# Last pair of attention heads run batch by batch, with separate homes for the second head's K and Q and the first head's output weight

## What is computed

```python
x = x + attn(_layernorm(x), ...)            # 32 heads of 128, K and Q normed over all heads
x = x + xattn(_layernorm(x), ctx_4096, ...) # fake-quantised product with the context
x = x + ffn(_layernorm(x), ...)             # base product + routed low-rank experts

# attn
q = rms_norm(h @ Wq + bq, gq); k = rms_norm(h @ Wk + bk, gk); v = h @ Wv + bv
attn = softmax(einsum('bhqd,bhkd->bhqk', q, k) * scale)
out  = einsum('bhqk,bhkd->bhqd', attn, v)   # 2 batches, 32 heads
return out @ Wo + bo

# xattn, one product per batch
q1 = clip(round(x1 / s1 + z1), 0, 255); q2 = clip(round(x2 / s2 + z2), 0, 255)
return matmul((q1 - z1) * s1, (q2 - z2) * s2)
```

## Time and profile before

| | us |
|---|---|
| median of 3 runs | 537.58 |
| lowest, highest | 535.88, 537.90 |
| the profiled execution | 537.49 |
| its span, first to last instruction | 535.6 |
| mean granted TensorE clock, share of full | 0.996 |

### The profile page before, as it was taken

How to read it: one execution, slowest core, us unless ns; L and a number is a source line. 1 busy time by engine, 2 the same in 40 slices (tenths; PEclk the granted TensorE clock), 3 DMA queues, 4 the chain that set the end, 5 groups by cost and what they waited for, 6 DMA issues and landing times.

```text
span 535.6 us, 9738 instructions
## 1 busy us (share of the span) xinstructions
PE 521.4 (97%) x3213; PEld 462.6 (86%) x3213; DVE 331.6 (62%) x696; ACT 354.8 (66%) x741; POOL 271.0 (51%) x228
## 2 busy tenths in 40 slices
PE   6999999999999999999999999999999999998997
PEld 5888888888888889999999999999999999986586
DVE  6254444266666667666666666666666666666855
ACT  3566666556666767767767776776777677677730
POOL 3344444364444446564646546464555646455440
PEclk8999999999999999999999999999999999999999
DMA  5444635232333221211222121121132412220002
GB/s 183 124 135 137 233 97 176 80 93 90 95 96 96 78 81 40 59 61 60 59 59 48 50 59 59 59 59 59 46 115 61 137 61 60 60 70 30 1 1 80
DMA packets 23494, 43.42 MB, mean 81 GB/s; under 512 B 3632, under 2 KB 3888, under 8 KB 23216
## 3 DMA queue, kind: packets, MB, share of 16 engines
q1 hardware_dynamic: 23472, 43.13, 26.7%
HBM read 41.03 MB, written 2.10 MB: 81 GB/s over the span
## 4 chain that ended last, share of the span: by engine, by line
PE 92%; DVE 4%; ACT 2%; DMA 1%; issue 0%; POOL 0%; SPq 0%; DVEq 0%
PE p_t L514 5%; PE p_v L593 5%; PE p_v L595 5%; PE p_t L515 5%; PE p_o L517 5%; PE p_o L515 5%; PE p_v L594 5%; PE p_o L514 5%; PE p_t L517 5%; PE acc L612 5%; PE acc L613 5%; PE acc L614 5%; PE p_t L579 5%; PE p_o L631 3%; PE p_o L633 3%; PE p_o L632 3%
## 5 line engine op out<-in xcount | busy, mean ns | idle before, releaser
L1102 DVE TENSOR_TENSOR w_lo<-raw,w_hi 128x512 fp32r<-128x512 f32 x64 | 44.2, 690 | 78.0 <-ACT w_hi L724 78.0
L969 POOL TENSOR_TENSOR wo_lo<-raw,wo_hi 128x512 fp32r<-128x512 f32 x31 | 40.1, 1293 | 100.5 <-ACT wo_hi L858 100.5
L724 ACT CAST w_hi<-raw 128x512 fp32r<-128x512 f32 x64 | 39.9, 623 | 67.6 <-PE p_t L517 30.3
L793 ACT ACTIVATE probs<-p_s,nbias,rq_t 128x256 f32<-128x256 f32 x128 | 71.3, 562 | 19.1 <-DVE nbias L1205 19.1
L593 PE MATMUL p_v<-w_hi,xnt_hi 128*128 128x256 f32 x256 | 77.2, 301 | 0.0
L595 PE MATMUL p_v<-w_hi,xnt_lo 128*128 128x256 f32 x256 | 72.3, 283 | 0.0
L594 PE MATMUL p_v<-w_lo,xnt_hi 128*128 128x256 f32 x256 | 72.2, 282 | 0.0
L951 POOL TENSOR_TENSOR acc_k<-acc_k,square 128x512 f32<-128x512 f32 x32 | 41.7, 1302 | 53.6 <-ACT square L739 53.6
L951 POOL TENSOR_TENSOR acc_q<-acc_q,square 128x512 f32<-128x512 f32 x32 | 43.5, 1360 | 40.2 <-ACT square L739 39.9
L842 ACT CAST pt_hi<-p_t 128x512 fp32r<-128x512 f32 x64 | 37.4, 584 | 38.8 <-PE p_t L579 38.8
L969 POOL TENSOR_TENSOR w_lo<-raw,w_hi 128x512 fp32r<-128x512 f32 x32 | 44.8, 1401 | 20.6 <-ACT w_hi L776 20.6
(11 more groups left out here) (275 smaller groups left out, 1487.0 us busy)
## 6 DMA issues: line engine op xcount, KB each, us to landing
raw<-in_wv SPq DMA_DIRECT2D x36, 256.0 KB, 2.6
raw<-in_wk SPq DMA_DIRECT2D x32, 256.0 KB, 2.6
raw<-in_wq SPq DMA_DIRECT2D x32, 256.0 KB, 2.6
raw<-in_wo SPq DMA_DIRECT2D x31, 256.0 KB, 2.6
ctx_f<-in_ctx SPq DMA_DIRECT2D x4, 512.0 KB, 3.6
xin<-in_x SPq DMA_DIRECT2D x4, 256.0 KB, 3.7
xb<-in_x SPq DMA_DIRECT2D x4, 256.0 KB, 6.1
ctx_kept<-ctx_k SPq DMA_DIRECT2D x1, 1024.0 KB, 5.1
```

The costliest lines, as they stand in the source:

```text
L793: act.activation(probs[:, b, a, :], p_s[:, a, :], ACT.Exp, bias=nbias[:, b, a:a + 1], scale=rq_t[:, 2 * b + a:2 * b + a + 1], accum_out=rs ...
L969: pool.tensor_tensor(dst, raw[:, slot, :], hi, ALU.subtract).then_inc(w_lo_pool, 1)
L1102: dve.tensor_tensor(w_lo[:, n, 0:NC * DH], raw[:, r, :], w_hi[:, n, 0:NC * DH], ALU.subtract).then_inc(w_lo_dve, 1)
```

## The change

All of it lies in pairs 14 and 15 and in what follows at once.

- Six tensors are added in dead heads of `k_all`: `k_31_hi`, `k_31_lo`, `q_31_hi`, `q_31_lo` for head 31, `wo_30_hi`, `wo_30_lo` for the output weight of head 30. The split of head 31's K and Q is moved from slot 60 to pair 14: ACT copies `k_31_hi` at the end of its second slot and `q_31_hi` at the end of its fourth, and POOL subtracts `k_31_lo`, `q_31_lo` there, each behind the `wo_lo` of that slot.
- The last pair (`last_pair`) runs its slots as (30, batch 0), (31, batch 0), (30, batch 1), (31, batch 1). So the scores for slot 61, issued first in slot 60, are now those of head 31.
- The output products of the two heads are made batch by batch as soon as a slot's output is split (`project_last(n)`), in halves of 128 x 256 for `o_hi` and `o_lo`. Batch 0 is complete in slot 62, and DVE takes its statistics, and the coefficients, inside the pair.
- `column_sums` go into `p_v` (inside slot 62) and `p_s` (after slot 63) in place of `p_t` and `p_s`. On ACT the second `column_part` stands behind `linear(0)` and `linear(1)`. On DVE the statistics of `acc2`, `acc3` stand behind `quantise(0)` and `quantise(1)`, and the last `o_last_lo` behind the coefficients of batch 0.

The core of the diff:

```diff
-            def scores(h, b):
-
-                s = 2 * h + b
-                if b == 0:
-                    pe.wait_ge(kq_lo, 2 * h + 2)
+            def scores(h, b, s=None):
+
+                kh, kl, qh, ql = k_hi, k_lo, q_hi, q_lo
+                if s is None:
+                    s = 2 * h + b
+                    if b == 0:
+                        pe.wait_ge(kq_lo, 2 * h + 2)
+                elif h == NH - 1:
+                    kh, kl, qh, ql = k_31_hi, k_31_lo, q_31_hi, q_31_lo
+                    pe.wait_ge(kq_31_lo, 2)
...
+            def last_pair():
+
+                for j in range(4):
+                    s = NS - 4 + j
+                    if j < 3:
+                        scores(NH - 2 + (j + 1) % 2, (j + 1) // 2, s + 1)
+                    transpose_probs(s, j % 2)
+                    if j < 2:
+                        project_out(NH - 3, j)
+                    if j > 0:
+                        project_last(j - 1)
+                    if j == 0:
+                        pe.wait_ge(v_lo_done, NH)
+                    if j == 2:
+                        column_sums(pe, 0)
+                    probs_v(s, j % 2, j // 2, 1, j % 2)
+                column_sums(pe, 1)
+                project_last(3)
...
+                    if peeled(p, NP - 2, NP - 1) and b == 1:
+                        src, to = ((k_all, k_31_hi), (q_all, q_31_hi))[j // 2]
+                        act.copy(to[:], src[:, NH - 1, :]).then_inc(kq_31_hi, 1)
...
+                    if peeled(p, NP - 2, NP - 1) and j % 2:
+                        src, hi, lo = ((k_all, k_31_hi, k_31_lo), (q_all, q_31_hi, q_31_lo))[j // 2]
+                        pool.wait_ge(kq_31_hi, 1 + j // 2)
+                        pool.tensor_tensor(lo[:], src[:, NH - 1, :], hi[:], ALU.subtract).then_inc(kq_31_lo, 1)
...
-            n = pair_stats(0)
...
             last_out_lo(1)
+            slot_max(NS - 1, 1, 1)
+            probs_lo(NS - 2)
+            stats1(0)
+            slot_norm(NS - 1, 1)
+
+            last_out_lo(2)
+            n = stats1(1)
+            probs_lo(NS - 1)
             pair_variance(0, n)
+            pair_coefficients(0)
+            last_out_lo(3)
             column_lo(0)
-            pair_coefficients(0)
-            n = pair_stats(1)
-            pair_variance(1, n)
             quantise(0)
             quantise(1)
+            stats1(2)
+            n = stats1(3)
+            pair_variance(1, n)
             pair_coefficients(1)
             column_lo(1)
```

More of the change, by code:

```diff
@@ L143, in decoder_layer @@
         bb_b = here("bb_b", [P, D], F32, k_at + 14 * KS)
+        wo_30_hi = here("wo_30_hi", [P, D], F32R, k_at + 5 * KS)
+        wo_30_lo = here("wo_30_lo", [P, D], F32R, k_at + 6 * KS)
+        k_31_hi = here("k_31_hi", [P, T], F32R, k_at + 7 * KS)
+        k_31_lo = here("k_31_lo", [P, T], F32R, k_at + 8 * KS)
+        q_31_hi = here("q_31_hi", [P, T], F32R, k_at + 9 * KS)
+        q_31_lo = here("q_31_lo", [P, T], F32R, k_at + 10 * KS)
         bm_f = here("bm_f", [P, D], F32, k_at + 15 * KS)
@@ L613, in project_out, with probs_v @@
                     pe.matmul(acc[t][:], ol[:, tt], wh[:], start=False, stop=False, skip_group_check=True)
-                    mm = pe.matmul(acc[t][:], oh[:, tt], wl[:], start=False, stop=last,
-                                   skip_group_check=True)
-                    if last:
+                    mm = pe.matmul(acc[t][:], oh[:, tt], wl[:], start=False, stop=(w == 1), skip_group_check=True)
+                    if w == 1:
                         mm.then_inc(x1_ready, 1)
[L618 to L623, removed]
+            def probs_v(s, within, b, par, half):
                 pe.wait_ge(pt_lo_done, s + 1)
@@ L634, in probs_v, with pair @@
                 mm.then_inc(pv_done, 1)
-            def pair(p, par, first=False, last=False):
+            def pair(p, par, first=False):
                 for j in range(4):
@@ L668, in _ @@
                 pair(p, p % 2)
[L669 to L673, removed]
+            last_pair()
             add_column_part(pe, 0)
@@ L830, in pair @@
                     if b == 0 and not peeled(h, 0, 1):
-                        act.wait_ge(pv_done, 2 * h)
-                        act.activation(o_hi[:], p_o[:], ACT.Identity, bias=column(bv_c, h - 1)
-                                       ).then_inc(o_hi_done, 1)
-                    if b == 0 and not (last and j == 2):
+                        head_out_hi(h)
+                    if b == 0:
                         act.wait_ge(scores_ready, 2 * h + 2)
@@ L1024, in _ @@
                 pair(p, p % 2)
-            pair(NP - 1, 1, last=True)
+            last_pair()
             for g in range(2):
@@ L1284, in _, with stats1 @@
                 pair(p, p % 2)
[L1285 to L1293 removed]
+            def stats1(t):
+                dve.wait_ge(x1_ready, t + 1)
+                return later(dve.bn_stats(stats[:, t, :], acc[t][:]))
             def pair_variance(g, n):
```

243 lines of the change are left out of this document (132 added, 111 removed).

## The result

| | median, us | runs | range, us | ratio to before, 95% interval |
|---|---|---|---|---|
| the kernel before | 536.25 | 7 | 535.88 to 537.90 | |
| the change | 538.84 | 7 | 538.21 to 540.66 | 1.0047 [1.0031, 1.0064] |
| the change, run again as e5 | 539.38 | 12 | 538.35 to 541.38 | 1.0059 [1.0042, 1.0076] |

The account below looks back on a forecast made before the run. TensorE's own work, busy 97% of the span, was taken as the bound, so only waits could move. -2.1 + 0.95 + 3.06 = 1.9, +0.4 behind the pair, +1.0 clock: +3.3 on 537.49 gives 540.8 us, range 538.9 to 542.0.

Parts of the forecast that it names:

- The base: Time of the profiled execution of the kernel before, 537.49 us, on which the predicted +3.3 was laid.
- second case: Rival: the wait before the last pair comes but the clock stays at 2.4 GHz; +2.3, 539.8 us; chance 0.33.
- Part 1: Pair 14: `k_31_lo` ahead of head 30's split makes `q_lo` late for its scores; wait 0.87, with refill 0.95 us.
- Part 2: Last pair's first scores: TensorE waits 3.06 us for `q_31_lo`, queued behind the second `wo_lo`; nothing hides it.
- Part 3: Last pair, first scores to first column part: 19.5 us in place of 21.58; the reorder itself gains 2.1.
- Part 4: Behind the pair: batch 1's late statistics delay the second `corr_lo` and second quantised product; delay grows 1.9 to 2.3.
- Part 5: Clock: the 3.06 us wait likelier than not drops TensorE's clock for 3.4 us; costs 1.0, bounds 0.6 to 1.7.
- The wait without a fall: Rival: wait before the last pair's first scores, clock staying at 2.4 GHz; +2.3, 539.8 us; chance 0.33.
- The split in time: Rival: `q_31_lo` done before TensorE asks, leaving the reorder's gain; about -1.0, 536.5 us; chance 0.05.
- More gets late: Rival: clock loss not absorbed (1.7), or `nbias` held through a second subtraction (1.25); +4.3, 541.8 us; chance 0.12.

Follow-up runs that it names:

- e3: The change with ten unused 128x512 matmuls on TensorE in front of the wait for head 31's split; 538.35 us, ratio 1.0038.
- e1: The change with head 31's K and Q splits at the end of the first and third slot of pair 14; 535.00 us, ratio 0.9975.
- e4: e1 with batch 1's `corr_lo` moved ahead of its coefficients on VectorE; 534.24 us, ratio 0.9962.
- e6: e4 with batch 0's column sums one slot earlier, in slot 61 instead of 62; 534.42 us, ratio 0.9966.
- e7: The change with head 31's K split at the end of pair 14's first slot, its Q split as in the change; 538.25 us, ratio 1.0024.
- e2: The kernel before, last pair in old order, with the four new homes and head 31's splits placed as in the change; 537.69 us, ratio 1.0020.

## Why the prediction missed, and where it was right

**The base: the step that failed.** The sum was made on 537.49, and the prediction checked that against the median of three, 537.58. Both came from executions above the usual: the kernel before takes 536.2 to 536.4 by every later set (7 to 32 runs each). So the base was 1.2 too high. The trace gave a sign of it: its 0.50 in the ninth to twelfth us was read as a measure of how long a fall lasts, and not as 0.9 us that this execution had lost and others might not; that the input came 0.43 late could not be seen from one trace. The median of three was bad luck as well, since 19 of the 84 later executions of that kernel lie over 537.3. On 536.25 the same range is 537.7 to 540.8, the forecast 539.6 and its second case 538.5; the two medians are 538.84 and 539.38. The execution of 538.84 has a mean clock of 0.999: it belongs to the second case, and the 1.0 that the sum adds for the clock is not in it.

**Part 1, right in kind, too small.** `q_lo` was late as said: the scores of head 30 are delayed by 0.66 from the first projection (473.71 - 11.39 against 474.23 - 12.58), where 0.87 to 0.95 was said, since the subtraction behind `wo_lo` starts after 1.24 and not 1.38, and TensorE starts 0.06 after the end of `q_lo` and not 0.14. Missed was the second wait, 0.7 more at the transposes, for the held norm: 1.4 in all, where the sum had 0.95. The prediction looked for a held VectorE instruction with two inputs in SBUF, `nbias`, at the place of the added subtraction, and `nbias` of that slot took 0.16 and was not held; it did not ask what the closed gap behind `q_lo` had been used for. The Trainium skill (SBUF — State Buffer, section Who interferes with whom) names `tensor_scalar` among the VectorE operations that can take the port pair shared with GpSimd, of which the later is blocked to the end of the other; the trace agrees, with 1.12 and 1.36 in place of 0.35 each.

**Part 2, right in kind, 0.3 too large.** TensorE went on 470.56 after the first projection, by the prediction 470.35. The wait is 2.62 as shown. The prediction's 3.06 counts from the time when the next matmul could start, which is 479.17 here (479.05 and the usual step of 0.12): 2.78. TensorE's greater delay does not shorten it, since `wo_hi` waits for TensorE and moves along (1.4 late as well); it is shorter by the step behind `wo_lo`, 1.23 and not 1.38, and by TensorE's start 0.05 after the end of `q_31_lo` and not 0.14. Sum of both parts: 4.2 against 4.0. That it comes so near is in part luck: 0.4 too little in part 1 and 0.3 too much here.

**Part 3, right.** From the first scores to the first column part 19.26 in e3, which has no fall, against 19.5. The single waits differ: 0.65 and 0.20 for the halves of `o_lo` in place of 0.88 and 0.52, and none is marked for `wo_30_lo` in e3 or the change, though about 0.3 of it is there: in e3 the projection that needs it starts 0.52 behind the matmul ahead (487.64, 488.16), where the usual step is 0.23, and 0.14 after `wo_lo` ended (488.02). There was no wait before the first column part, as said. The reorder gains 2.3 by e3 and 1.8 by e1, where the wait for `o_lo` of slot 60 stays.

**Part 4, right.** 0.5 in e3 (from 1.9 at the column part to 2.4 at the second product), against 0.4, and e4 shows by removal that it is `corr_lo` behind the coefficients.

**Part 5, right in kind; the size varies.** The fall was given odds of three to two, and a mean clock under 0.999 came in 14 executions of 19. It cost 0.8 in e5 (20.08 from scores to column part against 19.26) where 1.0 was said, and 2.05 in the first trace (21.31), above the upper bound of 1.7: the bound rested on a fall of 3.4 us, and this one lasted 6.9.

**The rivals.** The wait without a fall is the case of five executions, 538.21 to 538.84, 2.0 to 2.6 above the base where 2.3 was said. The split in time never came; e1 makes it come, and gives -1.2 where that rival said -1.0. "More gets late" came in two forms, the long fall and the held norm, though not the held `nbias` that it named. The measured ratio, 1.0047 and 1.0059, lies on the border of 0.5% that the chances were drawn at; the forecast's own ratio, 540.8 to 537.5, is 1.0061.

What stays open: why the same wait is followed by no fall, by one of 3.4 us or by one of 6.9 us, and why a wait of 1.01 us was followed by one in e6. No experiment shifted the wait in time while everything else stayed.

## What to carry to other kernels

Work that is copied ahead to a home of its own still has to pass an in-order queue: look where in that queue it stands, what is queued behind it, and which other engine lived in the gap that it closes. Here the same edit with the splits one slot earlier turns +2.6 into -1.2 us, and with one VectorE instruction moved, -1.9. Before a sum is laid on a profiled execution, look at its first stages for time that this one execution lost, and take more executions for the base: PEclk under 1.00 is one sign, but e7's trace started 2 us late with PEclk at 1.00, and only a second trace shows that.

## What the runs showed of the hardware

- Fp32 `tensor_scalar` on VectorE, 128x256 from SBUF to SBUF, took 0.35 us in the gaps of GpSimd and 1.12 and 1.36 us beside GpSimd subtractions that ran back to back; it ended 0.15 after each. In e2 it was 1.11 and 1.36, in e5 1.10 and 1.36.
- A wait of TensorE of 2.62 us with a busy TensorE on both sides was followed by 1.2 GHz in all three traces that have it (the change, where the fall began within the wait, e5 and e7), and by the mean clocks in 24 of 31 executions; one of 3.84 in all six. The fall lasted 3.4 us in one trace and 6.9 in another of the same kernel. In e6 one of 3.4 us began 1.8 us after a wait of 1.01 us. Ten unused matmuls, 2.46 us, kept the clock at 2.4 GHz in eleven of twelve executions by their mean clocks.
- The start of an execution moves by up to 2 us: the first projection matmul came at 11.0 to 11.4 us in nine traces, and at 12.58 and 13.06 in two.
